# Turning the expert tiles' activations on the DVE, in 32x32 blocks, in place of TensorE

## The chip, the cores and the metric

One core of a Trainium2 chip runs the whole program in one launch. The metric is device time in microseconds from the first to the last instruction of that core, the median of three runs. Engines are named as in the profile: PE is TensorE (matrix products), PEld its weight loads, DVE is VectorE, ACT is ScalarE, POOL is GpSimd, SP issues DMAs.

## The reference

A three-part layer on `x` of 8 x 256 tokens with 256 features, all in float32: a mixture of experts, a gated delta-rule attention, and the same mixture of experts once more. The change is in the two expert parts, which are:

```python
x_flat = x.reshape(-1, d)                      # 2048 tokens, d = 256
router_probs = softmax(x_flat @ gate_w)        # 8 experts
topk_w, topk_idx = top_k(router_probs, 2)      # two experts a token
topk_w = topk_w / sum(topk_w)
# rows sorted by expert, then for the rows of each expert:
h = silu(rows @ w1[e]) * (rows @ w3[e])        # 256 -> 896, twice
out = h @ w2[e]                                # 896 -> 256
# back to the tokens, weighted by topk_w, halved, added to x
```

In front of each part stands a layer norm.

## The kernel before

`build_ffn` first routes the tokens: it sorts the 4096 pairs of token and expert into 39 tiles of at most 128 rows (`TILES`), each of one expert. Then the expert loop runs over the tiles, in 13 groups of three (`GROUPS`, `RING = 3`), with three buffers of each tile in SBUF. All engines run the same order of tiles; what orders them against each other are semaphores, and each engine's order within a tile is written out by hand.

For one tile t the work is:

- POOL gathers 128 rows of normalized tokens from DRAM into `xg` with an indirect DMA (L491).
- PE turns `xg` with two transposes into PSUM (`turn_x`, L522), and ACT copies the result to `xgT` in SBUF (`copy_x`, L596).
- PE computes the up product in two halves of 448 columns (`up`, L533). Each half is eight passes: two weights, two slices of the contracted dimension, and two passes for a float32 product. The expert's weights lie in `wbuf`.
- ACT applies silu to one product (`silu`, L602); the DVE multiplies by the other (`gated`, L628). The result, `h`, has rows on partitions: 128 x 896.
- The down product contracts over the 896, so `h` has to be turned. PE turns it in seven blocks of 128 x 128 into two PSUM banks `ps_hT` (`turn_h`, L544); ACT copies four of them (`copy_h`, L606) and the DVE three (`copy_h`, L632) to `hT` in SBUF.
- PE computes the down product (`down`, L555), 14 passes of 256 columns.
- The DVE scales the result by the token's weight into `y` (`copy_y`, L639), and POOL adds it to the tokens' rows in DRAM with an indirect DMA (L500).

PE's order for tile t is: first up half of t, turns of h of t-1, second up half of t, turns of x of t+1, down product of t-1. The DVE's order is: first gate of t, copy of hT of t-1, second gate of t, copy of y of t-1. SP loads the weights of the next expert but one into the free half of `wbuf` as soon as `tiles_done` says that the expert before it is finished.

The semaphore `h_ready` counts finished gates, `hT_ready` finished copies of hT, `tiles_done` finished down products, `y_ready` finished copies of y.

Of the kernel before, what the change touches and what calls it, by code (L numbers as in the profile page):

```python
# [12 lines left out]
P = 128  # L13
# [6 lines left out]
MJ = M // P  # L20
# [4 lines left out]
RING = 3  # L25
# [15 lines left out]
BLK = 32  # L41
# [5 lines left out]
def at_least(eng, semaphore, value):  # L47

    if isinstance(value, int) and value <= 0:
        return  # L50
    eng.wait_ge(semaphore, value)
# [161 lines left out]
def build_ffn(nc, c, x, xnT, gate_w, w1, w2, w3, rows_in, sums, prefix, first):  # L213

    ctx = ExitStack()
    with ctx:
# [11 lines left out]
        with routing:  # L228
            q = Pools(nc, routing, prefix)
# [207 lines left out]
        with experts:  # L437
            q = Pools(nc, experts, prefix)
            xg = [q.sb(f"xg{b}", [P, D]) for b in range(RING)]
            xgT = [q.sb(f"xgT{b}", [P, KD, P]) for b in range(RING)]  # L440
            h = [q.sb(f"h{b}", [P, M]) for b in range(RING)]
            hT = [q.sb(f"hT{b}", [P, MJ, P]) for b in range(RING)]
            y = [q.sb(f"y{b}", [P, D]) for b in range(RING)]
            ps_up = [[q.ps(f"ps_up{hf}{k}", [P, 512]) for k in range(2)] for hf in range(2)]
            ps_hT = [q.ps(f"ps_hT{k}", [P, 512]) for k in range(2)]
            ps_xT = q.ps("ps_xT", [P, 512])
            ps_y = q.ps("ps_y", [P, 512])
            rows_loaded = [q.dma_sem(f"rows_loaded{b}") for b in range(RING)]
# [3 lines left out]
            up_ready = q.sem("up_ready")  # L452
            silu_ready = q.sem("silu_ready")
            h_ready = q.sem("h_ready")
            h_turned = q.sem("h_turned")
            hT_ready = [q.sem(f"hT_ready{k}") for k in range(2)]
            tiles_done = q.sem("tiles_done")
            slots_freed = q.sem("slots_freed")
            y_ready = q.sem("y_ready")
            GROUPS = TILES // RING  # L460
# [9 lines left out]
            with nc.Block() as block:  # L470
# [42 lines left out]
                @block.tensor  # L513
                def _(pe):
                    te = nc.tensor

                    def turn_x(i, b):
                        pe.wait_ge(rows_loaded[b], 16 * (i + 1))

                        at_least(pe, xT_ready, RING * i + b)  # L520
                        for k in range(KD):
                            last = te.transpose(ps_xT[:, P * k:P * k + P], xg[b][:, P * k:P * k + P], c["ident"][:])  # L522
                        last.then_inc(x_turned, 1)

                    def up(i, b, hf, off):
                        t = RING * i + b
                        if hf == 0:
                            pe.wait_ge(xT_ready, t + 1)

                        at_least(pe, h_ready, 2 * t + hf - 1)  # L530
                        for w in range(2):
                            for k in range(KD):
                                last = te.matmul(ps_up[hf][w][:, 0:MH], xgT[b][:, k, :],  # L533
                                                 wbuf[:, bass.ds(off + (w * WSIZE + k * M + hf * MH), MH)],
                                                 start=(k == 0), stop=(k == KD - 1))
                        last.then_inc(up_ready, 1)

                    def turn_h(i, b):
                        t = RING * i + b
                        pe.wait_ge(h_ready, 2 * t + 2)  # L540
                        for j in range(MJ):
                            if j % 4 == 0:
                                at_least(pe, hT_ready[j // 4], t)
                            last = te.transpose(ps_hT[j // 4][:, P * (j % 4):P * (j % 4) + P], h[b][:, P * j:P * j + P],  # L544
                                                c["ident"][:])
                            if j in (3, MJ - 1):
                                last.then_inc(h_turned, 1)

                    def down(i, b, off):
                        t = RING * i + b  # L550
                        for k in range(2):
                            pe.wait_ge(hT_ready[k], t + 1)
                        at_least(pe, y_ready, t)
                        for j in range(MJ):
                            last = te.matmul(ps_y[:, 0:D], hT[b][:, j, :],  # L555
                                             wbuf[:, bass.ds(off + (2 * WSIZE + j * D), D)],
                                             start=(j == 0), stop=(j == MJ - 1))
                        last.then_inc(tiles_done, 1)

                    def entry(i, b, k, low, high):  # L560
                        return pe.value_load(table[0:1, bass.ds(RING * i + b, 1), k:k + 1].rearrange("p a b -> p (a b)"),
                                             min_val=low, max_val=high)

                    def offset(i, b):
                        return entry(i, b, 0, 0, WSLOT)

                    def group(i, first_group, last_group):
                        for b in range(RING):
                            off = offset(i, b)
                            counts = [entry(i, b, 1 + k, 48, 48 * E // 2) for k in range(2)]  # L570
                            before = (i, b - 1) if b else (i - 1, RING - 1)
                            has = not (first_group and b == 0)
                            off_before = offset(*before) if has else None
                            for k in range(2):
                                pe.wait_ge(loaded[k], counts[k])
                            up(i, b, 0, off)
                            if has:
                                turn_h(*before)
                            up(i, b, 1, off)
                            if not (last_group and b == RING - 1):  # L580
                                turn_x(*((i, b + 1) if b < RING - 1 else (i + 1, 0)))
                            if has:
                                down(*before, off_before)

                    turn_x(0, 0)
                    grouped(pe, group)
                    turn_h(GROUPS - 1, RING - 1)
                    down(GROUPS - 1, RING - 1, offset(GROUPS - 1, RING - 1))

                @block.scalar  # L590
                def _(act):
                    sc = nc.scalar

                    def copy_x(i, b):
                        act.wait_ge(x_turned, RING * i + b + 1)
                        sc.copy(xgT[b][:].rearrange("p k m -> p (k m)"), ps_xT[:, 0:D]).then_inc(xT_ready, 1)  # L596

                    def silu(i, b, hf):
                        t = RING * i + b
                        act.wait_ge(up_ready, 2 * t + hf + 1)  # L600

                        sc.activation(h[b][:, MH * hf:MH * hf + MH], ps_up[hf][0][:, 0:MH], ACT.Silu).then_inc(silu_ready, 1)  # L602

                    def copy_h(i, b):
                        act.wait_ge(h_turned, 2 * (RING * i + b) + 1)
                        sc.copy(hT[b][:, 0:4, :].rearrange("p k m -> p (k m)"), ps_hT[0][:]).then_inc(hT_ready[0], 1)  # L606

                    def group(i, first_group, last_group):
                        for b in range(RING):
                            silu(i, b, 0)  # L610
                            if not (first_group and b == 0):
                                copy_h(*((i, b - 1) if b else (i - 1, RING - 1)))
                            silu(i, b, 1)
                            if not (last_group and b == RING - 1):
                                copy_x(*((i, b + 1) if b < RING - 1 else (i + 1, 0)))

                    copy_x(0, 0)
                    grouped(act, group)
                    copy_h(GROUPS - 1, RING - 1)

                @block.vector
                def _(dve):
# [4 lines left out]
                        part = h[b][:, MH * hf:MH * hf + MH]  # L627
                        v.tensor_tensor(part, part, ps_up[hf][1][:, 0:MH], ALU.mult).then_inc(h_ready, 1)  # L628

                    def copy_h(i, b):  # L630
                        dve.wait_ge(h_turned, 2 * (RING * i + b) + 2)
                        v.tensor_copy(hT[b][:, 4:MJ, :].rearrange("p k m -> p (k m)"),  # L632
                                      ps_hT[1][:, 0:(MJ - 4) * P]).then_inc(hT_ready[1], 1)

                    def copy_y(i, b):
                        dve.wait_ge(tiles_done, RING * i + b + 2)
# [4 lines left out]
                    def group(i, first_group, last_group):  # L641
                        for b in range(RING):
                            before = (i, b - 1) if b else (i - 1, RING - 1)
                            has = not (first_group and b == 0)
                            gated(i, b, 0)
                            if has:
                                copy_h(*before)
                            gated(i, b, 1)
                            if has:
                                copy_y(*before)  # L650

                    for i in range(GROUPS):
                        group(i, i == 0, i == GROUPS - 1)
                    copy_h(GROUPS - 1, RING - 1)
                    copy_y(GROUPS - 1, RING - 1)


# [1251 lines left out]
```

## Time and profile before

| | |
|---|---|
| Three runs | 3065.91, 3066.69, 3072.37 us; median 3066.69 |
| Profiled execution | span 3065.9 us, the same as the lowest of the runs |
| Mean granted clock of PE | 0.944 of full |
| Busy in the span | PE 2722.1 us (89%), DVE 1929.4 (63%), ACT 1384.1 (45%), POOL 703.5 (23%) |
| First expert loop | from about 78 to 478 us |
| Attention | from about 490 to 2560 us |
| Second expert loop | from about 2645 to 3044 us |

Times in the profile are microseconds from the start of the span, where not marked ns. An engine is busy while at least one of its instructions runs; overlapping instructions count once in the busy time, and the mean of one instruction is its own full duration. The granted clock is the share of its full rate that PE was given; its two levels are 1.2 and 2.4 GHz, 0.50 and 1.00.

### The profile page before, as it was taken

Reading aid. Unit: us, or ns where it says so; the run is one execution under the profiler, and the core shown is the slowest. Engines: PE = TensorE matmul, PEld = TensorE weight load, DVE = VectorE, ACT = ScalarE, POOL = GpSimd, SP = SyncE. Lnnn points to the kernel's source line nnn. Section 1 sums busy time; section 2 is a strip of 40 time slices with the busy share of each in tenths; the row PEclk is TensorE's granted clock in tenths of the full one; section 3 lists DMA queues with packets and bytes.
Section 4 is the critical chain, followed back from the end, with each engine's and each line's share of the span. In section 5 each row is a group of like instructions: output and inputs, shape, how many; then the busy total and the mean of one; then the engine's idle time right before and its main releaser. Section 6 shows DMA issues by size and latency. Waiting matters only on the chain. (4 is left out here: it accounts for less than half of the span.)

```text
span 3065.9 us, 58355 instructions
## 1 busy us (share of the span) xinstructions
PE 2722.1 (89%) x19346; PEld 2007.4 (65%) x19347; DVE 1929.4 (63%) x3648; ACT 1384.1 (45%) x4441; POOL 703.5 (23%) x954
## 2 busy tenths in 40 slices
PE   4999994556999999999999999999999995699996
PEld 4566663333677777777777777777777775566664
DVE  4122222588889889888898898898887543322221
ACT  0111111334666666666666666666665552111111
POOL 1222221322222222222221322213221111122221
PEclk7999996778999999999999999999999997699998
DMA  4223311345654544544545455455553321223322
GB/s 156 60 64 99 96 26 48 103 144 154 182 160 152 167 149 151 179 135 158 166 134 181 137 159 165 148 167 155 154 155 108 104 68 55 88 61 99 98 62 45
DMA packets 378125, 374.75 MB, mean 122 GB/s; under 512 B 213076, under 2 KB 293460, under 8 KB 377876
## 3 DMA queue, kind: packets, MB, share of 16 engines
q1 hardware_dynamic: 362900, 351.05, 36.4%
q0 software_dynamic: 14976, 20.46, 4.0%
q8 instruction: 147, 2.41, 0.3%
q14 instruction: 102, 0.84, 0.1%
HBM read 234.83 MB, written 138.67 MB: 122 GB/s over the span
## 5 line engine op out<-in xcount | busy, mean ns | idle before, releaser
L533 PE MATMUL f_ps_up<-f_wbuf,f_xgT 128*128 x1248 | 500.4, 544 | 5.4 <-issue 3.3
L628 DVE TENSOR_TENSOR f_h<-f_h,f_ps_up 128x448 f32<-128x448 f32 x156 | 96.9, 621 | 472.7 <-ACT f_h L602 472.7
L602 ACT ACTIVATE f_h<-f_ps_up 128x448 f32<-128x448 f32 x156 | 84.9, 544 | 636.3 <-PE f_ps_up L533 636.3
L533 PEld LDWEIGHTS f_ps_up<-f_wbuf,f_xgT 128*128 128x128 f32 x1248 | 231.7, 192 | 190.0 <-issue 185.3
L1265 PE MATMUL at_bank<-xnT,at_w_qk 128*128 128x512 f32 x512 | 273.6, 663 | 58.9 <-DVE at_qk L1589 55.5
L1589 DVE SCALAR_TENSOR_TENSOR at_qk<-at_bank,at_taps_qk,at_qk 128x510 f32<-128x510 f32 (+2 forms) x384 | 280.7, 744 | 46.2 <-ACT at_qk L1463 37.1
L1589 DVE SCALAR_TENSOR_TENSOR at_vT<-at_bank,at_taps_v,at_vT 128x510 f32<-128x510 f32 (+2 forms) x384 | 280.4, 744 | 36.0 <-ACT at_vT L1470 26.9
L1849 POOL TENSOR_SCALAR at_small<-at_small 128x4 f32<-128x4 f32 x64 | 17.4, 272 | 1215.1 <-ACT at_squares L1497 1215.1
L1443 PE MATMUL at_bank<-at_w_out,at_yT 128*128 128x256 f32 x1024 | 259.7, 402 | 36.2 <-issue 35.4
L500 POOL DMA_INDIRECT sums<-f_y,f_row_of x78 | 123.9, 1588 | 583.3 <-DVE f_y L639 583.3
L1290 PE MATMUL at_bank<-at_w_vz,xnT 128*128 128x256 f32 x1024 | 245.3, 383 | 9.0 <-DVE at_vT L1589 9.0
L555 PE MATMUL f_ps_y<-f_wbuf,f_hT 128*128 x1092 | 248.8, 379 | 1.6 <-DVE f_hT L632 1.6
L1443 PEld LDWEIGHTS at_bank<-at_w_out,at_yT 128*128 128x128 f32 x1024 | 197.6, 202 | 66.7 <-issue 41.2
L1278 PE MATMUL at_bank<-xnT,at_w_vz 128*128 128x512 f32 x512 | 231.8, 593 | 6.3 <-DVE at_qk L1589 2.3
L555 PEld LDWEIGHTS f_ps_y<-f_wbuf,f_hT 128*128 128x128 f32 x1092 | 201.5, 190 | 27.0 <-issue 2.8
L1497 ACT ACTIVATE at_squares<-at_bank 128x128 f32<-128x128 f32 x512 | 135.2, 282 | 172.8 <-PE at_bank L1301 171.5
L1290 PEld LDWEIGHTS at_bank<-at_w_vz,xnT 128*128 128x128 f32 x1024 | 185.5, 191 | 31.0 <-DVE at_vT L1589 10.8
L1265 PEld LDWEIGHTS at_bank<-xnT,at_w_qk 128*128 128x128 f32 x512 | 96.8, 209 | 147.4 <-issue 137.4
L1470 ACT ACTIVATE at_vT<-at_bank,at_taps_v 128x512 f32<-128x512 f32 x128 | 88.1, 688 | 189.1 <-PE at_bank L1278 189.1
L1278 PEld LDWEIGHTS at_bank<-xnT,at_w_vz 128*128 128x128 f32 x512 | 96.5, 190 | 103.6 <-issue 98.2
L1566 ACT ACTIVATE at_junk<-at_y 128x128 f32<-128x128 f32 x512 | 150.6, 299 | 0.3 <-DVE at_y L1766 0.3
L1517 ACT ACTIVATE at_vr<-at_bank,at_t_vscale 128x256 f32<-128x256 f32 x256 | 107.4, 471 | 93.3 <-PE at_bank L1322 93.3
(233 smaller groups left out, 5607.8 us busy)
## 6 DMA issues: line engine op xcount, KB each, us to landing
f_wbuf<-in_L_ffn_w_dram SPq DMA_DIRECT2D x48, 896.0 KB, 7.0
at_steps_e<-steps_kept SPq DMA_DIRECT2D x64, 512.0 KB, 6.7
pt_kept<-at_pt_made SPq DMA_DIRECT2D x64, 512.0 KB, 2.7
mt_kept<-at_mt_made SPq DMA_DIRECT2D x64, 512.0 KB, 4.3
at_mt<-mt_kept SPq DMA_DIRECT2D x64, 512.0 KB, 4.1
at_pt<-pt_kept SPq DMA_DIRECT2D x64, 512.0 KB, 4.6
qk_kept<-at_qk SPq DMA_DIRECT2D x64, 256.0 KB, 2.6
ks_kept<-at_ks_made SPq DMA_DIRECT2D x64, 256.0 KB, 2.7
```

The lines of the kernel that those rows point to most:

```text
L500: nc.gpsimd.indirect_dma_start(out=sums, out_offset=bass.IndirectOffsetOnAxis(ap=row_of[:, t:t + 1], axis=0), in_=y[t % RING][:], in_offse ...
L533: last = te.matmul(ps_up[hf][w][:, 0:MH], xgT[b][:, k, :], wbuf[:, bass.ds(off + (w * WSIZE + k * M + hf * MH), MH)], start=(k == 0), stop ...
L555: last = te.matmul(ps_y[:, 0:D], hT[b][:, j, :], wbuf[:, bass.ds(off + (2 * WSIZE + j * D), D)], start=(j == 0), stop=(j == MJ - 1))
L628: v.tensor_tensor(part, part, ps_up[hf][1][:, 0:MH], ALU.mult).then_inc(h_ready, 1)
L1265: last = te.matmul(proj_bank[ct][:], w_qk[u[0] % 2][:, k, ct * P:(ct + 1) * P], xnT[:, k, UT * u[1]:UT * u[1] + UT], start=(k == 0), stop= ...
L1278: last = te.matmul(proj_bank[v][:], w_vz[:, k, v * P:(v + 1) * P], xnT[:, k, UT * u[1]:UT * u[1] + UT], start=(k == 0), stop=(k == KD - 1))
L1290: last = te.matmul(proj_bank[half][:, 256 * t:256 * t + 256], xnT[:, k, bass.ds(UT * u[1] + P * (2 * half + t), P)], w_vz[:, k, 2 * P:4 * ...
L1443: last = te.matmul(proj_bank[half][:, 256 * t:256 * t + 256], yT[:, 2 * (2 * half + t) + v, :], w_out[:, v, :], start=(v == 0), stop=(v == ...
L1497: last = sc.activation(squares[:, t, :], src[:, P * t:P * t + P], ACT.Square, accum_out=small[two(u)][:, 4 * a + t:4 * a + t + 1])
L1517: last = sc.activation(vr[two(u)][:, 2 * t:2 * t + 2, :].rearrange("p n m -> p (n m)"), gen[1 + 2 * (t // 2)][:, 256 * (t % 2):256 * (t % ...
L1566: last = sc.activation(junk[:, n, :], y[two(u)][:, n, :], ACT.Square, accum_out=osum[two(u)][:, n:n + 1])
L1589: ins = v_.scalar_tensor_tensor(out=dst[:, :, back:], in0=src[:, :, 0:SEQ - back], scalar=taps[:, 3 - back:4 - back], in1=dst[:, :, back:] ...
```

## The change

The seven turns on PE, the two PSUM banks and both copies go. In their place the DVE turns `h` in SBUF, straight into `hT`. One instruction of the DVE takes 32 partitions of `h` and, for each of the seven groups of 128 columns, 32 columns; it turns each of the seven 32 x 32 blocks. Sixteen such instructions (four row blocks by four column blocks) make the whole tile, and the last one raises `hT_ready`, which is now one semaphore. Reads start at partition 32 x `rows`, writes at partition 32 x `cols`. In the DVE's order the new step stands behind `copy_y` of the tile before.

```diff
-            ps_hT = [q.ps(f"ps_hT{k}", [P, 512]) for k in range(2)]
-            h_turned = q.sem("h_turned")
-            hT_ready = [q.sem(f"hT_ready{k}") for k in range(2)]
+            hT_ready = q.sem("hT_ready")
 # tensor engine
-                    def turn_h(i, b):
-                        ...
-                            last = te.transpose(ps_hT[j // 4][:, P * (j % 4):P * (j % 4) + P], h[b][:, P * j:P * j + P],
-                                                c["ident"][:])
                     def down(i, b, off):
                         t = RING * i + b
-                        for k in range(2):
-                            pe.wait_ge(hT_ready[k], t + 1)
+                        pe.wait_ge(hT_ready, t + 1)
 # tensor engine, in the loop over tiles
                             up(i, b, 0, off)
-                            if has:
-                                turn_h(*before)
                             up(i, b, 1, off)
 # scalar engine: copy_h and its calls removed
 # vector engine
-                    def copy_h(i, b):
-                        ...
+                    def turn_h(i, b):
+                        t = RING * i + b
+                        dve.wait_ge(h_ready, 2 * t + 2)
+                        at_least(dve, tiles_done, t - RING + 2)
+                        for rows in range(P // BLK):
+                            for cols in range(P // BLK):
+                                src = h[b][BLK * rows:BLK * rows + BLK, :].rearrange("p (j m) -> p j m", m=P)[:, :, BLK * cols:BLK * cols + BLK]
+                                last = v.transpose(hT[b][BLK * cols:BLK * cols + BLK, :, BLK * rows:BLK * rows + BLK], src)
+                        last.then_inc(hT_ready, 1)
 # vector engine, in the loop over tiles
                             gated(i, b, 0)
-                            if has:
-                                copy_h(*before)
                             gated(i, b, 1)
                             if has:
                                 copy_y(*before)
+                            turn_h(i, b)
```

## Rows read from the trace of the kernel before

**Rows 1.** The page: busy time by engine, and one DMA issue (KB, us to landing).

```profile
PE 2722.1 (89%) x19346; PEld 2007.4 (65%) x19347; DVE 1929.4 (63%) x3648; ACT 1384.1 (45%) x4441; POOL 703.5 (23%) x954
...
f_wbuf<-in_L_ffn_w_dram SPq DMA_DIRECT2D x48, 896.0 KB, 7.0
```

**Rows 2.** Windows, first expert loop: length; busy us (count) of PE, PEld, DVE, ACT, POOL; clock.

```profile
200.00:300.00 100.00, 100.00 (x390) 65.33 (x389) 21.92 (x40) 18.30 (x40) 25.79 (x20) 1.00 0.33 87
```

**Rows 3.** Timeline of one tile: start, duration, engine, instructions, idle time before.

```profile
271.51 3.17 PE L533 MATMUL f_ps_up<-f_wbuf,f_xgT 128*128 x8
...
274.51 0.93 PE L544 MATMUL f_ps_hT<-ident,f_h 128*128 128x128 f32 x7
...
275.28 3.17 PE L533 MATMUL f_ps_up<-f_wbuf,f_xgT 128*128 x8
275.29 0.62 DVE L628 TENSOR_TENSOR f_h<-f_h,f_ps_up 128x448 f32<-128x448 f32 x1 [3.10 <-ACT f_h L602]
...
275.83 0.55 DVE L632 COPY f_hT<-f_ps_hT 128x384 f32<-128x384 f32 x1
...
278.29 0.38 PE L522 MATMUL f_ps_xT<-ident,f_xg 128*128 128x128 f32 x2
...
278.50 3.19 PE L555 MATMUL f_ps_y<-f_wbuf,f_hT 128*128 x14
...
281.53 3.17 PE L533 MATMUL f_ps_up<-f_wbuf,f_xgT 128*128 x8
```

**Rows 4.** Timeline of the last tile of the second expert loop.

```profile
3038.52 0.48 DVE L639 TENSOR_SCALAR f_y<-f_ps_y,f_weight_of 128x256 f32<-128x256 f32 x1 [1.83 <-PE f_ps_y L555]
...
3039.29 0.56 DVE L632 COPY f_hT<-f_ps_hT 128x384 f32<-128x384 f32 x1 [0.28 <-PE f_ps_hT L544]
...
3040.05 3.28 PE L555 MATMUL f_ps_y<-f_wbuf,f_hT 128*128 x14 [0.80 <-DVE f_hT L632]
3043.37 0.48 DVE L639 TENSOR_SCALAR f_y<-f_ps_y,f_weight_of 128x256 f32<-128x256 f32 x1 [3.53 <-PE f_ps_y L555]
```

**Rows 5.** DVE instructions by line and shape: count, busy us, mean ns of one.

```profile
L180 DVE TENSOR_SCALAR f_xn<-x,f_mv,f_rstd 128x256 f32<-128x256 f32 x32 | 10.5, 405 | 7.0 <-POOL f_rstd L168 7.0
...
L1666 DVE TENSOR_REDUCE at_half_way<-at_terms 128x64 f32<-128x256 f32 x16 | 6.7, 420 | 0.6
L1727 DVE COPY at_w_low<-at_w_up 128x256 f32<-128x256 f32 x16 | 6.1, 380 | 0.0
...
L349 DVE MATCH_VALUE_LOAD f_best_at<-f_best,f_probs 128x8 f32 x32 | 2.4, 74 | 0.1
...
L894 DVE TENSOR_SCALAR at_t_g<-tab_a 128x512 f32<-128x512 f32 x1 | 0.4, 427 | 0.0
```

**Rows 6.** Timeline of the DVE in the attention stage.

```profile
1505.41 4.52 DVE L1589 SCALAR_TENSOR_TENSOR at_qk<-at_bank,at_taps_qk,at_qk 128x510 f32<-128x510 f32 x6
1509.96 0.69 DVE L1748 TENSOR_SCALAR at_xb<-at_bank 64x512 f32<-64x512 f32 x1
1510.69 0.69 DVE L1781 TENSOR_TENSOR x<-x,at_bank 128x512 f32<-128x512 f32 x1
...
1526.68 0.68 DVE L1766 TENSOR_TENSOR at_y<-at_bank,at_o_state 128x512 f32<-128x512 f32 x1
1527.28 0.41 DVE L1748 TENSOR_SCALAR at_xb<-at_bank 128x256 f32<-128x256 f32 x1
```

**Rows 7.** Timeline of the start of the first expert loop.

```profile
90.30 0.62 DVE L628 TENSOR_TENSOR f_h<-f_h,f_ps_up 128x448 f32<-128x448 f32 x1 [2.38 <-ACT f_h L602]
...
101.23 0.48 DVE L639 TENSOR_SCALAR f_y<-f_ps_y,f_weight_of 128x256 f32<-128x256 f32 x1 [2.04 <-PE f_ps_y L555]
```

**Rows 8.** A window of the attention stage, columns as in rows 2.

```profile
1500.00:1580.00 80.00, 74.97 (x628) 58.43 (x627) 73.36 (x138) 51.27 (x171) 21.07 (x34) 1.00 0.47 149
```

**Rows 9.** Timeline of PE in that window: its longest idle time.

```profile
1507.92 1.97 PE L1443 MATMUL at_bank<-at_w_out,at_yT 128*128 128x256 f32 x8 [2.52 <-issue]
```

More of the change, by code:

```diff
@@ L536, in up @@
                         last.then_inc(up_ready, 1)
-                    def turn_h(i, b):
[L539 to L543, printed above, removed]
-                            last = te.transpose(ps_hT[j // 4][:, P * (j % 4):P * (j % 4) + P], h[b][:, P * j:P * j + P],
-                                                c["ident"][:])
-                            if j in (3, MJ - 1):
-                                last.then_inc(h_turned, 1)
                     def down(i, b, off):
                         t = RING * i + b
-                        for k in range(2):
-                            pe.wait_ge(hT_ready[k], t + 1)
+                        pe.wait_ge(hT_ready, t + 1)
                         at_least(pe, y_ready, t)
@@ L586, in _ @@
                     grouped(pe, group)
-                    turn_h(GROUPS - 1, RING - 1)
                     down(GROUPS - 1, RING - 1, offset(GROUPS - 1, RING - 1))
@@ L602, in silu @@
                         sc.activation(h[b][:, MH * hf:MH * hf + MH], ps_up[hf][0][:, 0:MH], ACT.Silu).then_inc(silu_ready, 1)
-                    def copy_h(i, b):
-                        act.wait_ge(h_turned, 2 * (RING * i + b) + 1)
-                        sc.copy(hT[b][:, 0:4, :].rearrange("p k m -> p (k m)"), ps_hT[0][:]).then_inc(hT_ready[0], 1)
                     def group(i, first_group, last_group):
@@ L610, in group @@
                             silu(i, b, 0)
-                            if not (first_group and b == 0):
-                                copy_h(*((i, b - 1) if b else (i - 1, RING - 1)))
                             silu(i, b, 1)
@@ L618, in _ @@
                     grouped(act, group)
-                    copy_h(GROUPS - 1, RING - 1)
                 @block.vector
@@ L628, in gated @@
                         v.tensor_tensor(part, part, ps_up[hf][1][:, 0:MH], ALU.mult).then_inc(h_ready, 1)
[L630 to L633, printed above, removed]
+                    def turn_h(i, b):
[7 more added lines that the diff above has]
+                        last.then_inc(hT_ready, 1)
                     def copy_y(i, b):
@@ L650, in group @@
                                 copy_y(*before)
+                            turn_h(i, b)
                     for i in range(GROUPS):
                         group(i, i == 0, i == GROUPS - 1)
-                    copy_h(GROUPS - 1, RING - 1)
                     copy_y(GROUPS - 1, RING - 1)
```

## The prediction

> **What bounds the kernel now.** I read the page's busy shares first [rows 1]: TensorE is busy in 89% of the span and the DVE in 63%, but these are means over three stages. The windows come next, since the change touches only the two expert stages: there [rows 2] TensorE is busy 100.00 of 100 us at a granted clock of 1.00 (its upper level, 2.4 GHz), the DVE 21.9 and ScalarE 18.3. Then the timeline of one tile [rows 3] gives the period. The first half of the up product (eight passes) begins at 271.51 and for the next tile at 281.53 us, so a tile takes 10.02 us, and on TensorE it is: first up half 271.51 to 274.51 (3.00), the seven turns of h 274.51 to 275.28 (0.77), second up half to 278.29 (3.01), the next tile's x turned to 278.50 (0.21), down product to 281.53 (3.03). TensorE waits for nobody, so the stage is TensorE's own sum. The DVE's copy (L632, 0.55) lies beside the second up half, and so does ScalarE's.
>
> **What is removed.** The turns give TensorE back 0.77 us of the 10.02, so its own sum falls to 9.25. The copy of ScalarE costs nothing today and gives nothing back: ScalarE is busy 18.3% of the stage [rows 2]. The DVE's copy gives it 0.55 us.
>
> **What is added, and where.** Sixteen transposes per tile on the DVE, each 32 partitions by 224 elements, placed after copy_y of the tile before. That order makes a loop through two engines: copy_y(t-1) waits for down(t-1); turn_h(t) stands behind copy_y(t-1); down(t) waits for turn_h(t) (hT_ready); and copy_y(t) waits for down(t). If d is the time from one transpose's start to the next's, one turn of this loop is copy_y 0.48, a start gap of 0.03, 16 d, and then the way from a finished hT to the next copy_y. This last piece is in the trace, at the stage's end, the one place where TensorE already waits for hT [rows 4]: the DVE's copy ends at 3039.29 + 0.56 = 3039.85, the down product starts at 3040.05 and lasts 3.28, copy_y starts at 3043.37, together 3.52 us. The loop is thus 0.48 + 0.03 + 3.52 + 16 d = 4.03 + 16 d. The gates (L628, two of 0.62) queue behind turn_h on the DVE, but they run while down does (1.24 in 3.28 us), and the next up half needs only the first of them. A period is the larger of TensorE's 9.25 and this loop: TensorE sets it up to d = 0.326 us, the old 10.02 is reached at d = 0.374. So all hangs on d, sixteen times a tile.
>
> **The cost of d.** No transpose of the DVE is in the trace. Per element the DVE takes (621 - 420)/192 = 1.05 ns, by a product of 448 elements against a reduction of 256 [rows 3, 5], so 224 elements are 0.23 us and the rest is a fixed part. A block's first output column needs all 32 columns of its input, so 32 more elements pass first: a transpose of 224 should last about as long as a plain instruction of 256. Rows of 256 elements from one SBUF operand [rows 5]: a copy with its axes swapped 0.380 us, a two-scalar operation 0.405, a reduction 0.420. I take 0.405, the middle. Below: the copy without the 32, 0.380 - 0.034 = 0.346. Above: half the rate, which is a plain instruction of 448 elements, 0.621 (L628, [rows 3]).
>
> The second half of d is whether neighbours overlap, and here the trace speaks clearly. In the attention stage [rows 6] L1748 comes in two forms. The one on 128 partitions starts at 1527.28, 0.08 before its predecessor's end (1526.68 + 0.68). The one on 64 partitions writes and reads from partition 64 on; it starts at 1509.96, 0.03 after its predecessor's end (1505.41 + 4.52), and its successor, back at partition 0, starts 0.04 after its end. The rows shown stand for all: of the 64-partition form 54 of 64 follow a busy DVE, and all 54 start 0.02 to 0.04 late; all 64 of the other form overlap by 0.06 to 0.09. So an instruction whose first partition differs from its predecessor's waits for it to end. In turn_h the output's first partition changes with every instruction (the inner loop runs over cols) and the input's with every fourth. I therefore add 0.03 to each rather than take 0.08 off: d = 0.405 + 0.03 = 0.435.
>
> The Trainium skill has this as a rule ("VectorE: DVE Perf Modes", section "Two Vector instructions with no wait between them"): an instruction is held until all earlier ones have finished if its output starts in another 32-partition quadrant than the last output did. The trace agrees, by the 54 starts above; with the rule the loop is 10.99 us, without it (0.405 - 0.08) 9.31. The same page, in "The three transpose paths", gives 311 ns for a 128x128 bf16 transpose, which as an estimate for 96 elements more would be about 0.41 us, d about 0.44 and the total some 3159; no run here shows it yet.
>
> **The sum.** Loop: 4.03 + 16 x 0.435 = 10.99, which is 0.97 over the old period and 1.74 over TensorE's own sum, so TensorE now waits 1.7 us a tile before down. Per stage of 39 tiles: from copy_y(0) to copy_y(37) are 37 periods, 37 x 0.97 = 35.9. At the end copy_y(37) to copy_y(38) was 3043.37 - 3038.52 = 4.85 [rows 4], since the turns and copies overlapped the down before; now it is a whole loop, 10.99: +6.1. At the start [rows 7] gated(0, 1) ends at 90.92, so copy_y(0) comes at 90.92 + 0.03 + 6.96 + 3.52 = 101.43 instead of 101.23: +0.2. That is 42.2 a stage (in general 39 times the change of period plus 4.4), 84.4 for both. On the span of 3065.9 it makes 3150.3; that span equals the lowest of the three times, so nothing lies around it, and the median stands 0.8 above it: **3151 us**.
>
> Costed at nothing: POOL's scatter and gather, 25.8 us in ten tiles [rows 2], are due a whole tile later, and the gathers run ahead by up to three tiles; if that cover went, 2.6 us would still fit in the 9.25. The weight loads land 7.0 us after issue [rows 1] while an expert has some five tiles, 50 us. Fifteen more instructions a tile on the DVE have to be issued; no row prices that, but its shortest instruction (L349) takes 0.074 [rows 5], far below d, so issue should hide behind execution.
>
> **Rivals.**
> (a) Faster: the transposes overlap, or stream two elements at a time. Then d is 0.405 - 0.08 = 0.325, or, from the scalar operation whose 512 elements take only 0.427 [rows 5], less its 288 extra elements at half of 1.05 ns each, 0.28 + 0.03 = 0.31. Up to d = 0.326 TensorE sets the pace: 37 x 0.77 + 0.77 back per stage, less the longer end (loop of about 9 for 4.85, +4.1), 25 a stage, so 3016 us. It decides from d below 0.367, where 39 periods' gain pays the 4.4 of the end. Against it stand the 54 held starts. Chance 0.09.
> (b) Half rate for 4-byte elements, or fill and drain of each block not overlapped: d = 0.621 + 0.03 = 0.651, loop 14.45, 78 x 4.43 + 8.8 = +354: 3421 us. Nothing in the trace speaks for or against; 0.08.
> (c) The clock falls in the new gap. If down ran at the lower level, its 3.03 would double and the loop grow by 3.03 x 78 = 236 on top: some 3387 us. Against it: between 1500 and 1580 us TensorE idled 5.0 of 80 us, 2.52 of it in one piece, at a granted 1.00 [rows 8, 9]. 0.03.
> (d) The forecast with an extra step in each instruction: one more short instruction (L349), 0.074 [rows 5], makes d 0.51, loop 12.19, +178: 3245 us. 0.12.
>
> **How the numbers follow.** The forecast, a held transpose at full rate with 0.346 to about 0.43, has 0.68. Its low end is d = 0.376, loop 10.05, +11: 3078. With (d) above it, 3078 to 3245 holds 0.80. A measurement of this kernel tells about 0.2%, 6 us, from no change. Faster needs (a), 0.09, and a bit for shorter fixed parts: 0.10. The same needs d between 0.362 and 0.372: 0.03. Slower: 0.87.
>
> **What the changed profile would show.** Right: in the expert windows TensorE's busy share falls from 100 to about 84 with the clock still 1.00; its idle time stands before the down product, released by the DVE's f_hT, about 1.7 us a tile; transposes start about 0.435 apart, with a gap and not an overlap; the DVE's busy time rises to about 8.2 of 11.0 us a tile; the attention stage keeps its length. Wrong: starts under 0.33 apart and TensorE at 100 (a); transposes near 0.6 (b); a granted clock below 1 (c).

## The result

The change makes the kernel slower: 3125.15 us (median of four runs, 3119.27 to 3137.21) against 3068.32 before (four runs), a ratio of 1.0184, 95% interval 1.0161 to 1.0208. The prediction was 3151 with a range of 3078 to 3245. The profiled execution took 3125.36 us, of which its span is 3123.6; so 1.8 us lie around the span, where the prediction had assumed nothing.

The page of the changed kernel, its busy times (to [rows 1]) and the groups of the two products and of the transposes (busy us, mean ns, idle time before them):

```profile
PE 2701.1 (86%) x18800; PEld 1955.2 (63%) x18801; DVE 2385.5 (76%) x4818; ACT 1346.2 (43%) x4363; POOL 704.4 (23%) x954
...
L531 PE MATMUL f_ps_up<-f_wbuf,f_xgT 128*128 x1248 | 493.6, 549 | 68.1 <-issue 61.3
L613 DVE STREAM_TRANSPOSE f_hT<-f_h 32x224 f32<-32x224 f32 x1248 | 501.7, 402 | 16.0
...
L541 PE MATMUL f_ps_y<-f_wbuf,f_hT 128*128 x1092 | 258.3, 389 | 22.7 <-DVE f_hT L613 22.2
```

A transpose lasts 402 ns, and 1248 of them are busy 501.7 us: 402 ns each, so no two overlap. TensorE, which waited for nobody before, now stands idle some 90 us ahead of its two products, and three quarters of it (68.1) are ahead of up and not of down.

The windows of the expert stage (to [rows 2], same columns) show that the clock stayed at its upper level, and that TensorE's busy share fell to 91% and not to the 84% that the prediction named:

```profile
200.00:300.00 100.00, 91.19 (x306) 55.27 (x305) 75.27 (x178) 12.97 (x29) 23.24 (x18) 1.00 0.34 94
...
2760.00:2860.00 100.00, 91.18 (x300) 54.39 (x300) 76.53 (x182) 12.70 (x28) 25.49 (x20) 1.00 0.31 81
```

And the timeline of some tiles (to [rows 3]), from one copy_y (L620) over the transposes (L613) and the down product (L541) to the next:

```profile
99.24 0.48 DVE L620 TENSOR_SCALAR f_y<-f_ps_y,f_weight_of 128x256 f32<-128x256 f32 x1 [2.28 <-PE f_ps_y L541]
99.64 6.63 DVE L613 STREAM_TRANSPOSE f_hT<-f_h 32x224 f32<-32x224 f32 x16
...
99.80 6.28 PE L531 MATMUL f_ps_up<-f_wbuf,f_xgT 128*128 x16 [0.60 <-issue]
...
106.31 1.15 DVE L604 TENSOR_TENSOR f_h<-f_h,f_ps_up 128x448 f32<-128x448 f32 x2
...
106.42 3.28 PE L541 MATMUL f_ps_y<-f_wbuf,f_hT 128*128 x14
...
109.74 0.48 DVE L620 TENSOR_SCALAR f_y<-f_ps_y,f_weight_of 128x256 f32<-128x256 f32 x1 [2.28 <-PE f_ps_y L541]
...
138.04 3.28 PE L541 MATMUL f_ps_y<-f_wbuf,f_hT 128*128 x14
...
141.36 0.48 DVE L620 TENSOR_SCALAR f_y<-f_ps_y,f_weight_of 128x256 f32<-128x256 f32 x1 [2.13 <-PE f_ps_y L541]
...
141.76 6.63 DVE L613 STREAM_TRANSPOSE f_hT<-f_h 32x224 f32<-32x224 f32 x16
...
142.74 6.28 PE L531 MATMUL f_ps_up<-f_wbuf,f_xgT 128*128 x16 [1.42 <-issue]
...
149.07 3.19 PE L541 MATMUL f_ps_y<-f_wbuf,f_hT 128*128 x14
...
152.29 0.48 DVE L620 TENSOR_SCALAR f_y<-f_ps_y,f_weight_of 128x256 f32<-128x256 f32 x1 [2.05 <-PE f_ps_y L541]
```

From 99.24 to 109.74 the loop is closed: copy_y, the sixteen transposes, 0.15 us, down, copy_y, 10.50 us. The sixteen take 6.63, so d = (6.63 - 0.40)/15 = 0.415. From 141.36 to 152.29 it is 10.93, and another chain ends last: hT is ready at 148.39, but TensorE begins its up product only at 142.74, 1.42 us after down, and comes to down at 149.07. Of the 74 periods inside the two stages 54 are 10.50 to 10.62 and 20 are 10.89 to 10.93: every third one, where TensorE's loop goes from one group of three tiles to the next.

By the starts of copy_y the 57.7 us between the two spans come from these places: 22.0 and 22.0 from the 37 periods of each stage (370.7 and 392.7 us), 7.5 and 8.2 from the last step of each (4.85 before, 12.34 and 13.02 now), 0.1 from all that lies between the stages, and -2.0 from the start: the first up product took 7.66 us instead of 8.90, at a granted clock of 0.79 between 78 and 90 us instead of 0.66, and began 0.6 earlier. That is chance: in the other nine profiled runs of this document it took 8.1 to 8.9 us, whatever the kernel.

### The profile page after: what moved, and what is told of

It is laid out like the page before. It is cut to its first block and busy times, and to the rows that moved or that the text cites. A ratio compares the mean times of both kernels' runs of the same rounds, so it can differ in the third digit from the quotient of the medians.

```text
span 3123.6 us, 58259 instructions
## 1 busy us (share of the span) xinstructions
PE 2701.1 (86%) x18800; PEld 1955.2 (63%) x18801; DVE 2385.5 (76%) x4818; ACT 1346.2 (43%) x4363; POOL 704.4 (23%) x954
## 5 line engine op out<-in xcount | busy, mean ns | idle before, releaser
L531 PE MATMUL f_ps_up<-f_wbuf,f_xgT 128*128 x1248 | 493.6, 549 | 68.1 <-issue 61.3
L613 DVE STREAM_TRANSPOSE f_hT<-f_h 32x224 f32<-32x224 f32 x1248 | 501.7, 402 | 16.0
L541 PE MATMUL f_ps_y<-f_wbuf,f_hT 128*128 x1092 | 258.3, 389 | 22.7 <-DVE f_hT L613 22.2
L541 PEld LDWEIGHTS f_ps_y<-f_wbuf,f_hT 128*128 128x128 f32 x1092 | 204.2, 193 | 59.9 <-issue 31.9
L620 DVE TENSOR_SCALAR f_y<-f_ps_y,f_weight_of 128x256 f32<-128x256 f32 x78 | 37.7, 483 | 177.5 <-PE f_ps_y L541 177.5
L1760 DVE TENSOR_TENSOR x<-x,at_bank 128x512 f32<-128x512 f32 x128 | 87.8, 686 | 90.4 <-PE at_bank L1422 89.9
```

The lines of the kernel that those rows point to most:

```text
L531: last = te.matmul(ps_up[hf][w][:, 0:MH], xgT[b][:, k, :], wbuf[:, bass.ds(off + (w * WSIZE + k * M + hf * MH), MH)], start=(k == 0), stop ...
L541: last = te.matmul(ps_y[:, 0:D], hT[b][:, j, :], wbuf[:, bass.ds(off + (2 * WSIZE + j * D), D)], start=(j == 0), stop=(j == MJ - 1))
L613: last = v.transpose(hT[b][BLK * cols:BLK * cols + BLK, :, BLK * rows:BLK * rows + BLK], src)
L1760: v_.tensor_tensor(dst, dst, proj_bank[half][:], ALU.add).then_inc(s["added"], 1)
```

## The experiments

Ratios are to the kernel before, run on the same chip. Periods are from one copy_y to the next, by the timeline.

**The DVE's order: is it the loop through copy_y?** (`e1_turn_first`)

```diff
                             gated(i, b, 1)
+                            turn_h(i, b)
                             if has:
                                 copy_y(*before)
-                            turn_h(i, b)
```

> Only the DVE's order changes: turn_h(t) ahead of copy_y(t-1) instead of behind it. Theory: the period of 10.5 us is a loop (copy_y waits for down, turn_h stands behind copy_y, down waits for turn_h). With turn_h ahead the loop is open: the DVE's work is 6.63 + 1.24 + 0.48 = 8.35 us a tile, under TensorE's 9.25, and hT is ready about 8 us after the tile's up product, 1.5 us before down wants it. Expected: period 9.25 to 9.6 us, total 3016 to 3045 us, faster than the kernel before. Rival 1: the DVE's sixteen transposes themselves, or what they take from others in SBUF, set the pace: then the order does not matter and it stays near 3125. Rival 2: TensorE's late issue of the next up product (0.4 to 1.4 us, put down to issue in the changed kernel) comes with the missing turns and not with the wait: period about 10.1, total about 3080.

Measured: 3057.43 us, ratio 0.9948 (0.9932 to 0.9965). The same transposes, as long as before (403 ns), and the kernel is now faster than the one with TensorE's turns; so rival 1 falls, and the loop is shown: it was the place of turn_h behind copy_y that cost the time. The size was missed by 12 us at least. The periods go 9.25, 9.84 and about 10.1 in turn, and the timeline of TensorE says why:

```profile
214.72 3.19 PE L541 MATMUL f_ps_y<-f_wbuf,f_hT 128*128 x14
218.23 6.28 PE L531 MATMUL f_ps_up<-f_wbuf,f_xgT 128*128 x16 [0.32 <-issue]
224.34 0.38 PE L520 MATMUL f_ps_xT<-ident,f_xg 128*128 128x128 f32 x2
224.56 3.19 PE L541 MATMUL f_ps_y<-f_wbuf,f_hT 128*128 x14
228.19 1.01 PE L531 MATMUL f_ps_up<-f_wbuf,f_xgT 128*128 x2 [0.44 <-issue]
```

Down no longer waits for hT. But the up product after it is late by 0.32 and 0.44 us, although all its data are there. The amount is about that of rival 2, but not for its reason: in `e4_four_wide` below the turns are missing as well, and there no up product is late. Down waits for one thing more here, which the expectation overlooked: for `copy_y` of the tile before, by `y_ready`. In this order that copy ends 0.5 us after hT is ready (213.83 and 213.32 us). What these 0.5 us cost no run tells.

**The loop over groups written out** (`e2_unrolled`, with the order of the change)

```diff
-                group(0, True, False)
-                with eng.Fori(1, GROUPS - 1) as i:
-                    group(i, False, False)
-                group(GROUPS - 1, False, True)
+                for i in range(GROUPS):
+                    group(i, i == 0, i == GROUPS - 1)
```

> The changed kernel with TensorE's and ScalarE's loop over the 11 middle groups of three tiles written out instead of run as a hardware loop. In the changed kernel two periods of three are 10.50 us and the third, between two groups, 10.90, with 1.4 us of issue before the up product. Theory: the third is the loop's branch and what is read after it, exposed because TensorE's sequencer stood at the wait for hT and could not run ahead; written out, all periods are 10.50: 22 times 0.4, so 9 us less, about 3116. Rival: the late issue is the four reads of the tile's table entries, the same in each tile, and the branch adds nothing: 3125, unchanged.

Measured: 3118.88 us, ratio 1.0148 (1.0127 to 1.0169). All 74 periods are 10.50 or 10.51, so the 10.9 of every third one (20 places, not the 22 of the expectation) came from the hardware loop. The interval overlaps that of the change itself (from 1.0161 on); it is the trace that settles it, here by two starts of copy_y (L618):

```profile
208.52 0.48 DVE L618 TENSOR_SCALAR f_y<-f_ps_y,f_weight_of 128x256 f32<-128x256 f32 x1 [2.28 <-PE f_ps_y L539]
...
219.02 0.48 DVE L618 TENSOR_SCALAR f_y<-f_ps_y,f_weight_of 128x256 f32<-128x256 f32 x1 [2.28 <-PE f_ps_y L539]
```

How much of it is the branch isn't shown. Written out, every address and count that depended on the loop's `i` is a constant too, and up comes earlier in two tiles of three, not only at the branch. The idle time of TensorE ahead of up, first three tiles of the changed kernel and then two of this one:

```profile
195.49 6.28 PE L531 MATMUL f_ps_up<-f_wbuf,f_xgT 128*128 x16 [0.82 <-issue]
...
206.56 6.28 PE L531 MATMUL f_ps_up<-f_wbuf,f_xgT 128*128 x16 [1.38 <-issue]
...
216.51 6.28 PE L531 MATMUL f_ps_up<-f_wbuf,f_xgT 128*128 x16 [0.44 <-issue]
```
```profile
198.40 6.28 PE L529 MATMUL f_ps_up<-f_wbuf,f_xgT 128*128 x16 [0.42 <-issue]
...
219.46 6.28 PE L529 MATMUL f_ps_up<-f_wbuf,f_xgT 128*128 x16 [0.48 <-issue]
```

**One quadrant for all: is a transpose held?** (`e3_one_quadrant`)

```diff
-                                src = h[b][BLK * rows:BLK * rows + BLK, :]...
-                                last = v.transpose(hT[b][BLK * cols:BLK * cols + BLK, :, BLK * rows:BLK * rows + BLK], src)
+                                src = h[b][0:BLK, :]...
+                                to = hT[b] if cols == 0 else spare[cols - 1]
+                                last = v.transpose(to[0:BLK, :, BLK * rows:BLK * rows + BLK], src)
...
```

The lines not shown make the three spare tiles, clear hT ahead of the loop, and let the DVE wait for its own turns of the tile before.

> The sixteen transposes of a tile all read from partitions 0 to 31 and write to partitions 0 to 31 (twelve of them into spare tiles), same size and count; so hT holds only a part of what it should. Theory: a transpose is held by its predecessor because its first partition differs; with one quadrant for all, each starts 0.08 us before its predecessor ends: starts 0.32 apart instead of 0.415, the sixteen in 5.2 us instead of 6.63, loop about 9.0, and TensorE sets the pace: 3020 to 3070 us. Rival: transposes never overlap, whatever the quadrant: starts stay 0.415 apart and the total near 3125.

Measured: 3047.64 us, ratio 0.9917 (0.9897 to 0.9937). The timeline of the DVE, four transposes from one start in hT to the next:

```profile
207.23 0.94 DVE L617 STREAM_TRANSPOSE f_spare<-f_h 32x224 f32<-32x224 f32 x3
208.11 0.36 DVE L617 STREAM_TRANSPOSE f_hT<-f_h 32x224 f32<-32x224 f32 x1
208.40 0.94 DVE L617 STREAM_TRANSPOSE f_spare<-f_h 32x224 f32<-32x224 f32 x3
209.28 0.36 DVE L617 STREAM_TRANSPOSE f_hT<-f_h 32x224 f32<-32x224 f32 x1
```

Starts lie (209.28 - 208.11)/4 = 0.29 apart instead of 0.415. The same size and number, only the first partitions of input and output no longer change: being held costs 0.12 us an instruction, 2.0 us a tile. In the changed kernel twelve of the fifteen steps from one transpose to the next change the output's first partition alone, and their starts are as far apart (0.40 to 0.42 us) as those of the other three; so a change of the output's is enough. That is the rule of the Trainium skill that the prediction weighed ("VectorE: DVE Perf Modes", section "Two Vector instructions with no wait between them"), and this run bears it out directly. With it gone, TensorE set the pace, with periods of mostly 9.25 to 9.8; in the longer ones its up product is late by 0.2 to 0.3 us, as in the run before.

**Four wide instructions: does time go by partitions?** (`e4_four_wide`)

```diff
-                        for rows in range(P // BLK):
-                            for cols in range(P // BLK):
-                                ...
+                        for cols in range(P // BLK):
+                            part = slice(BLK * cols, BLK * cols + BLK)
+                            src = h[b][:].rearrange("p (j m) -> p j m", m=P)[:, :, part]
+                            last = v.transpose(hT[b][:, :, part], src)
```

> Four transposes of 128 partitions by 224 elements in place of sixteen of 32 partitions: each 32x32 block is turned, but stays in its own 32 partitions, so the blocks of hT off the diagonal are not where they belong. Theory: an instruction's time goes by elements per partition and not by partitions: each lasts 0.40 us, four of them 1.4 to 1.7, loop under 6 us, TensorE sets the pace at 9.25 to 9.6: 3016 to 3045 us. Rival: the time goes by the data moved, then each lasts up to 1.6 us and the total stays near 3125.

Measured: 3010.71 us, ratio 0.9805 (0.9785 to 0.9826). By the group of the transposes and one tile's row in the timeline:

```profile
L613 DVE STREAM_TRANSPOSE f_hT<-f_h 128x224 f32<-128x224 f32 x312 | 99.9, 377 | 0.1
```
```profile
212.46 1.28 DVE L613 STREAM_TRANSPOSE f_hT<-f_h 128x224 f32<-128x224 f32 x4
```

Four times the data in an instruction of 377 ns, against 357 for one of 32 partitions that isn't held either (`e3_one_quadrant`): the time goes by elements per partition. All 74 periods are 9.25 to 9.31 except the last of each stage (9.03), which is TensorE's own sum as predicted. The real work isn't done this way: the blocks off the diagonal would have to change their 32 partitions.

**Each transpose in two pieces** (`e5_halves`, one run)

```diff
-                                last = v.transpose(hT[b][BLK * cols:BLK * cols + BLK, :, BLK * rows:BLK * rows + BLK], src)
+                                dst = hT[b][BLK * cols:BLK * cols + BLK, :, BLK * rows:BLK * rows + BLK]
+                                v.transpose(dst[:, 0:5, :], src[:, 0:5, :])
+                                last = v.transpose(dst[:, 5:MJ, :], src[:, 5:MJ, :])
```

> The changed kernel with each transpose cut into one of five blocks (160 elements) and one of two (64), which follow each other with the same partitions. Theory: a transpose costs a fixed part and 1.04 ns an element, and only a change of quadrant holds: the second of a pair starts 0.06 us before the first ends, the first of the next pair 0.01 after; a pair takes about 0.52 us instead of 0.415, so the period grows by 1.7 us to 12.2 and the time to about 3255 us. Rival: the time goes by elements alone: pairs take 0.42 us, period 10.5, 3125 us.

Measured: 3193.33 us in one run, between the two forecasts. The mechanism holds, the sum in the expectation was too high:

```profile
210.27 0.33 DVE L614 STREAM_TRANSPOSE f_hT<-f_h 32x160 f32<-32x160 f32 x1
210.54 0.19 DVE L615 STREAM_TRANSPOSE f_hT<-f_h 32x64 f32<-32x64 f32 x1
210.75 0.34 DVE L614 STREAM_TRANSPOSE f_hT<-f_h 32x160 f32<-32x160 f32 x1
```
```profile
L614 DVE STREAM_TRANSPOSE f_hT<-f_h 32x160 f32<-32x160 f32 x1248 | 418.4, 335 | 15.6
L615 DVE STREAM_TRANSPOSE f_hT<-f_h 32x64 f32<-32x64 f32 x1248 | 241.5, 194 | 0.0
```

The second piece starts 0.06 before the first ends (same partitions), the next first piece after a gap (other partitions); a pair takes 0.48, and the period is 11.47. Of 160 elements a held transpose lasts 335 ns, of 224 402: 67/64 = 1.05 ns an element and a fixed 0.17 us. The second pieces, which are not held, last 194: by the same 1.05 ns an element their fixed part is 0.13.

**Both edits, and then the table's entries** (`e6_both`, `e7_entries_first`)

The first has the order of `e1_turn_first` and the loop of `e2_unrolled`; the second also this:

```diff
                         for b in range(RING):
-                            off = offset(i, b)
-                            counts = [entry(i, b, 1 + k, 48, 48 * E // 2) for k in range(2)]
+                            if first_group and b == 0:
+                                fetch(0, 0)
+                            off, counts = read[i, b]
...
-                            off_before = offset(*before) if has else None
+                            off_before = read[before][0] if has else None
...
                                 turn_x(*((i, b + 1) if b < RING - 1 else (i + 1, 0)))
+                            if not (last_group and b == RING - 1):
+                                fetch(*((i, b + 1) if b < RING - 1 else (i + 1, 0)))
                             if has:
                                 down(*before, off_before)
```

`fetch` reads a tile's weight offset and its two load counts into `read`.

> turn_h(t) ahead of copy_y(t-1) as in the run with the DVE's order changed (3057 us, periods 9.25, 9.84 and 10.1 in turn), and TensorE's and ScalarE's loop over the groups written out. Theory: only what the third period has over the second, some 0.3 us at 22 places, is the loop's branch: about 3050 us, periods 9.25 to 9.85. Rival: without the branch the sequencer always keeps ahead: all periods 9.25, about 3020 us.

> As the last one, and TensorE reads the next tile's table entries (weight offset and two load counts) ahead of its wait for hT and the down product, instead of behind them; the offset for down is kept from the earlier reading. Theory: what makes the up product late is that its entries are read only after the wait for hT has let the sequencer go on; read before it, they cost nothing: all periods 9.25 to 9.35, 3015 to 3030 us, about 1.5% under the kernel before. Rival: the time from hT to the next up product is the issue of down's 28 instructions: no change against the run without it, about 3050 us.

Measured: 3036.00 us, ratio 0.9901 (0.9880 to 0.9921), and 3022.53 us, ratio 0.9844 (0.9829 to 0.9858). In the first the periods lie between 9.25 and 9.8 after the first one (10.35), short and long mostly in turn: writing the loop out was worth more than the theory gave the branch, and it was still not all. In the second all are 9.25 to 9.27 except the first of each stage (9.5), and its timeline has no idle time on TensorE:

```profile
209.20 3.19 PE L539 MATMUL f_ps_y<-f_wbuf,f_hT 128*128 x14
212.22 6.18 PE L529 MATMUL f_ps_up<-f_wbuf,f_xgT 128*128 x16
218.24 0.38 PE L518 MATMUL f_ps_xT<-ident,f_xg 128*128 128x128 f32 x2
218.45 3.19 PE L539 MATMUL f_ps_y<-f_wbuf,f_hT 128*128 x14
221.48 6.18 PE L529 MATMUL f_ps_up<-f_wbuf,f_xgT 128*128 x16
```

So what made the up product late was that the sequencer read the table's entries only after its waits ahead of down. Three of the four readings are moved and the fourth, down's offset once more, is dropped; what each is worth isn't told apart. This version is 1.6% faster than the kernel before.

**The same two edits without the DVE's transposes** (`e8_before_read`: the kernel before, the loop written out, the entries read ahead)

> The kernel before, with TensorE's turns, and only the two edits of the fastest version that have nothing to do with the DVE: the loop over groups written out, and the next tile's table entries read ahead of the wait for hT. Theory: before the change TensorE never waited and its sequencer was always ahead, so these edits give nothing: periods 10.02, within 0.3% of 3067 us. The gain of the fastest version over the kernel before is then that of the removed turns. Rival: the edits are worth the 1.5% by themselves: about 3022 us.

Measured: 3069.12 us, ratio 0.9992 (0.9981 to 1.0002). No change: where TensorE never waits, its sequencer is ahead anyway. The 1.6% come from taking the turns off TensorE, once nothing holds it up.

## Why the prediction was right, and where its sizes were off

**The bound and its exchange.** Right. TensorE's own sum fell to 9.25 (`e4_four_wide`, `e7_entries_first`), and the new loop through copy_y, turn_h and down took over at 10.50. Opening it at one place turned 1.8% loss into 0.5% gain. TensorE's idle time inside the stages is about 1.0 us a tile, not 1.7.

**The duration of a transpose.** 0.405 predicted from rows of 256 elements, 0.402 measured, and in part that is luck. The row of 0.405 (L180) is one whose instructions overlap; sixteen of them in the kernel before:

```profile
19.68 5.26 DVE L180 TENSOR_SCALAR f_xn<-x,f_mv,f_rstd 128x256 f32<-128x256 f32 x16 [3.53 <-POOL f_rstd L168]
```

Their starts are (5.26 - 0.405)/15 = 0.32 apart, so none is held. Transposes that overlap in the same way last 0.357:

```profile
L617 DVE STREAM_TRANSPOSE f_spare<-f_h 32x224 f32<-32x224 f32 x936 | 294.0, 357 | 0.0
```

The estimate for a transpose that isn't held was thus 0.05 too long, and the hold, which the sum had only as a gap, adds 0.045 to the duration; the two cancel. So the step "224 elements and 32 more that have to pass first" isn't borne out by the 0.402; these runs don't show whether the fixed part holds such 32 elements. By the Trainium skill ("VectorE: DVE Perf Modes", section "The three transpose paths"), from its 311 ns for a 128x128 bf16 transpose, the prediction had an estimate of about 0.41. The held transposes come near it with 0.402, those that overlap don't with 0.357; no run has a bf16 one. Rival (b), half rate, is out by the slope of 1.05 ns an element, and rival (d), 0.51 from start to start, by the measured 0.415.

**The hold.** Right in kind, and the reason why rival (a) did not come. As a whole it was priced well: 0.435 held against 0.325 overlapping, 0.11 us, and measured 0.415 against 0.29, 0.12. But some of it lies in the duration, as said, and the sum's own term for it was too large: the gap between transposes is 0.415 - 0.402 = 0.013, not 0.03. With 16 in a tile that is the largest miss of the sum, 0.3 us of a loop of 10.99. Part of it was in the counting: sixteen transposes have fifteen gaps between them, and the sum took sixteen (its 9.31 without the rule does take fifteen).

**The rest of the loop.** Two smaller terms were too large as well. The first transpose starts 0.40 us after copy_y's start and overlaps its end, where the sum had 0.48 + 0.03; both write from partition 0 of SBUF on, and by the prediction's own rows such a pair overlaps. From the sixteenth transpose's end to the next copy_y are 3.47 us, not 3.52. With 16 x 0.02 for the gap and the duration this is the 0.49 us between 10.99 and 10.50. At 10.50 the rule of the prediction (39 times the change of period and 4.4, twice) gives +46 us.

**What the prediction did not have.** About +12 us more were measured, from two terms without a place in the sum. First, the late issue: at 20 of 74 periods 0.4 us, 8 us. The prediction said that TensorE's idle time would stand ahead of down, released by hT; three quarters of it stand ahead of up, because the sequencer held up at the wait for hT could no longer run ahead (`e7_entries_first`; and in `e4_four_wide`, where hT is ready some 4 us before down begins, no up product is late). Second, the end of each stage: 12.34 and 13.02 us for the last loop instead of 10.50, together 4.4. There TensorE is idle for 7.2 us, and the clock falls (windows as before):

```profile
492.00:499.00 7.00, 0.00 (x0) 0.00 (x0) 6.76 (x17) 0.00 (x0) 1.55 (x1) 0.79 0.17 19
499.00:504.00 5.00, 4.89 (x14) 3.87 (x14) 0.00 (x0) 0.00 (x0) 0.00 (x0) 0.61 0.00 0
```
```profile
499.11 5.12 PE L541 MATMUL f_ps_y<-f_wbuf,f_hT 128*128 x14 [7.22 <-DVE f_hT L613]
```

The last down product takes 5.12 us where it took 3.28 in [rows 4]; in the second loop it takes 5.81. Rival (c) was right about the mechanism at this one place; in the loop, with idle times of 0.4 to 1.4 us, the clock stayed at 1.00.

**The overall size.** Loop +46, late issue +8, the two ends +4, the luckier start -2 and rounding make the 57.7 of the spans; the forecast of 84 was too high by the loop's 0.49 us at 78 places, 38, less the 12 it left out.

## What to carry to other kernels

Before work is moved from a full engine to an idle one, draw the loop that the new order closes: an engine that is busy 76% can set the period if its new step stands behind a wait for the engine that needs its result. Put the step ahead of that wait first; here it was the difference between +1.8% and -0.5%. And once a sequencer has to wait, look at what it reads behind the wait: here that came late, and reading the next step's entries ahead of it made the kernel 0.4% faster still (3036.0 to 3022.5 us).

## What the runs showed of the hardware that was not expected

- A DVE transpose that is held by another does not only start later, it also lasts longer: the same transpose of 32 x 224 takes 402 ns when its partitions change and 357 (mean of 936 in `e3_one_quadrant`) when they don't. Held starts are 0.415 apart, the others 0.29. It isn't the change of partitions within an instruction: in `e5_halves` the second pieces go between the same partitions as the first, and their fixed part is 0.13 us, not 0.17. The rule is not complete: the first transpose of a tile, which overlaps the copy_y before it, lasts 390 in `e3_one_quadrant`.
- A transpose of 32 partitions costs about as much as one of 128 (357 in `e3_one_quadrant`, 377 in `e4_four_wide`, neither held).
- From a finished hT to TensorE's next up product 4.53 us pass in the changed kernel, from 106.27 to 110.80, of which TensorE is idle for 1.10 behind down. With the DVE's order turned, the loop written out and the entries read ahead of the wait, nothing of this idle time is left.
